# A hand-ordered two-attention decoder block: the last two groups of the first attention packed closer, batch 0's second maxima set behind them, batch 1's middle stage set earlier

## What is computed

```python
x = x + attn(layernorm(x))        # 16 heads of 8, scores = q.k + q.pe_k[clip(j-i)], softmax,
                                  # ctx = attn.v + attn.pe_v[clip(j-i)], then W_out and bias
y = layernorm(x)
# new memory = ctx_1024 shifted against y: a convolution (rate 4) over the old memory, then y itself
x = x + cross(ctx_1024, y)
src = layernorm(x)
# the block: q, k, v by W_q, W_kc W_k, W_vc W_v, rotary embedding, softmax(q.k), W_o, rmsnorm,
# a shared swiglu and 8 experts in 2 groups (the best group, its top 2), rmsnorm
x = x + ffn(src)
```

## Time and profile before

| what | value |
|---|---|
| median of 3 runs | 417.42 us (417.29 to 420.8) |
| profiled execution | 415.42 us, span 413.6 us, 1.8 us around it |
| PE busy | 356.1 us (86% of the span) |
| DVE busy | 297.4 us (72%) |
| ACT busy | 232.8 us (56%) |
| POOL busy | 162.4 us (39%) |
| mean granted clock of PE | 0.92 of full speed |

### The profile page before, as it was taken

One profiled execution on the slowest core, in us unless ns is written; L12 is line 12 of the kernel. 1 busy time (PEld: TensorE's weight loads), 2 busy tenths in 40 slices (PEclk: granted clock), 3 DMA queues, 4 the chain that ended last, 5 costly groups with the idle time before them and its releaser, 6 DMA issues.

```text
span 413.6 us, 12788 instructions
## 1 busy us (share of the span) xinstructions
PE 356.1 (86%) x5267; PEld 188.8 (46%) x5267; DVE 297.4 (72%) x538; ACT 232.8 (56%) x489; POOL 162.4 (39%) x342
## 2 busy tenths in 40 slices
PE   7667789898999999897889898769989898899993
PEld 4233356675676677654555332311333333453441
DVE  5998747777678788788799789566787661436465
ACT  2724656767666757565744567455867695422200
POOL 7264555456477576554470111200001161143423
PEclk9995559999999999999999699965999899999997
DMA  7400000000000001000000000500000000000000
GB/s 235 133 22 4 4 4 5 6 4 6 23 7 4 6 6 30 4 4 2 3 5 2 4 24 2 164 3 1 2 2 1 2 3 2 0 1 0 2 25 26
DMA packets 11991, 8.08 MB, mean 20 GB/s; under 512 B 4446, under 2 KB 11022, under 8 KB 11806
## 3 DMA queue, kind: packets, MB, share of 16 engines
q1 hardware_dynamic: 11934, 7.27, 6.1%
HBM read 5.94 MB, written 0.52 MB: 16 GB/s over the span
## 4 chain that ended last, share of the span: by engine, by line
PE 57%; DVE 22%; issue 7%; ACT 6%; POOL 3%; SPq 2%; DMA 2%; ACTq 0%; POOLq 0%; DVEq 0%
PE ps L1213 8%; PE ps L1308 7%; PE ps L1127 5%; PE ps L1158 5%; PE ps L1176 5%; DVE m_qk L850 4%; PE ps L1139 4%; PE ps L1185 4%; PE ps L1200 3%; PE ps L1097 3%; PE ps L1003 3%; ACT arena L683 3%; DVE m_qk L847 2%; PE ps L1294 2%; SPq L383 2%
## 5 line engine op out<-in xcount | busy, mean ns | idle before, releaser
L847 DVE TENSOR_REDUCE m_qk<-ps 128x2 f32<-128x1024 f32 x64 | 76.8, 1220 | 19.5 <-PE ps L1097 19.3
L850 DVE TENSOR_REDUCE m_qk<-ps 128x2 f32<-128x1024 f32 x64 | 76.9, 1219 | 15.9 <-PE ps L1185 15.5
L683 ACT ACTIVATE arena<-ps 128x512 f32<-128x512 f32 x128 | 69.4, 594 | 23.5 <-PE ps L1139 22.8
L698 ACT ACTIVATE arena<-ps 128x512 f32<-128x512 f32 x128 | 67.2, 590 | 21.2 <-PE ps L1200 20.9
L598 POOL TENSOR_TENSOR arena<-arena,eb 128x256 f32<-128x256 f32 x64 | 47.0, 734 | 62.4 <-ACT eb L671 31.6
L671 ACT ACTIVATE eb<-ps 128x512 f32<-128x512 f32 (+1 forms) x64 | 31.3, 542 | 30.3 <-PE ps L1127 30.3
L441 POOL TENSOR_SCALAR var<-mv 128x1 f32<-128x1 f32 (+1 forms) x14 | 2.7, 193 | 106.3 <-ACT eb L740 69.8
L1213 PE MATMUL ps<-arena,v_sb 128*20 128x256 f32 x512 | 41.2, 415 | 2.4 <-DVE arena L855 2.4
L1158 PE MATMUL ps<-arena,v_sb 128*20 128x128 f32 x1024 | 40.3, 284 | 0.0
L599 POOL TENSOR_TENSOR arena<-arena,eb 128x192 f32<-128x192 f32 x64 | 38.6, 603 | 0.0
L1200 PE MATMUL ps<-q_op,k_op 50*128 50x512 bf16 x128 | 31.9, 414 | 4.8 <-ACT arena L698 4.0
(11 more groups left out here) (217 smaller groups left out, 523.8 us busy)
## 6 DMA issues: line engine op xcount, KB each, us to landing
rel_v<-in_relv_ext SPq DMA_DIRECT2D x1, 1024.0 KB, 8.9
eb<-in_w SPq DMA_DIRECT2D x2, 512.0 KB, 5.3
x_sb<-in_x SPq DMA_DIRECT2D x2, 256.0 KB, 3.2
q_op<-farT SPq DMA_DIRECT2D x32, 3.0 KB
q_op<-farT SPq DMA_DIRECT2D x32, 1.5 KB
out<-x_sb SPq DMA_DIRECT2D x8, 64.0 KB, 1.5
rows<-in_rows SPq DMA_DIRECT2D x1, 448.0 KB, 6.7
sel<-in_sel SPq DMA_DIRECT2D x1, 384.0 KB, 4.2
```

Source lines behind the costliest of these rows:

```text
L683: act.activation(p_ring[:, k % SLOTS_P, e, :], ps[:, bank, :], ACT.Exp).then_inc(sm["bank_free"], 1)
L698: act.activation(p_ring[:, v % RING, e, :], ps[:, bank, :], ACT.Exp).then_inc(sm["bank_free"], 1)
L847: dve.tensor_reduce(m_qk[:, u, n:H:PAIRS], ps[:, banks, :], AX_X, ALU.max).then_inc(sm["pair_free"], 1)
L850: dve.tensor_reduce(m_qk[:, IT * b + n, 2 * p:2 * p + 2], ps[:, banks, :], AX_X, ALU.max).then_inc(sm["pair_free"], 1)
```

## The change

Only numbers of the plan change; every step is still there once, with the same instructions.

- Group 7: `bias` at 8, 9.5, 11, 12.5 (before 8, 11, 14, 17), `scores` one each step from 15 to 22 (before 15 to 25), `pv` from 21.6 to 25 (24 to 28), `crel` from 25.6 (29), and its `turn`, `fin`, `norm`, `back` some 5.5 steps sooner. Group 6: `crel` from 30.3 in steps of 0.7 (before 31 in steps of 1). Group 5: `fin`, `norm`, `back` ten steps sooner (97 and not 107).
- Batch 0: the four `again` six steps later (from 104.8 and not 98.5), `max2` from 108.5 (before 102.6), `sc2` from 118.5 (116).
- Batch 1: the middle stage from 116 (122), `max2` from 140.5 (139), `sc2` from 150.5 (147.5).
- `FRONT_AT` (output projection and gates of batch 0) 154.5 (152) and `LAST` 186.5 (183.5), three steps later with the end of `sc2`.

```diff
+BIAS_LAST = (8, 9.5, 11, 12.5)
+SCORES_LAST = (15, 16, 17, 18, 19, 20, 21, 22)
+CREL_EARLY = (30.3, 31, 31.7, 32.4)
...
-PV_LAST = (24, 24, 25, 25, 26, 26, 28, 28)
-MID_AT = (78, 122)
-MAX2_AT = (102.6, 139)
-SC2_AT = (116, 147.5)
+PV_LAST = (21.6, 21.6, 22.2, 22.2, 23, 23, 25, 25)
+CREL_LAST = (25.6, 26.2, 26.8, 27.4)
+MID_AT = (78, 116)
+MAX2_AT = (108.5, 140.5)
+SC2_AT = (118.5, 150.5)
 PV2_LAST = (1, 1.5, 2, 2.5, 3, 3.5, 4, 4.5)
-FRONT_AT = 152
-LAST = 183.5
+FRONT_AT = 154.5
+LAST = 186.5
...
+        bias_at, scores_at, pv_at = (BIAS_AT, SCORES_AT, PV_AT) if u < NT - 1 else (BIAS_LAST, SCORES_LAST, PV_LAST)
+        crel_at = CREL_AT if u < NT - 2 else (CREL_EARLY, CREL_LAST)[u - NT + 2]
+        plan += [(t + bias_at[q], 2, "bias", u, q) for q in range(4)]
+        plan += [(t + scores_at[p], 2, "scores", u, p) for p in range(PAIRS)]
         plan += [(t + pv_at[k], 6, "pv", u, k) for k in range(8)]
-        plan += [(t + CREL_AT[q] - early, 7, "crel", u, q) for q in range(4)]
-        plan += [(t + 35 - early, 0, "ctx", u, 0)]
+        plan += [(t + crel_at[q], 7, "crel", u, q) for q in range(4)]
+        plan += [(t + crel_at[3] + (1 if u < NT - 2 else 0.5), 0, "ctx", u, 0)]
         if u == NT - 1:
-            plan += [(t + 33.6, 1.5, "turn", u, 0), (t + 34.2, 5, "fin", u, 0), (t + 35.5, 1.5, "norm", u, 0), (t + 37, 4, "back", u, 0)]
+            plan += [(t + 28.2, 1.5, "turn", u, 0), (t + 28.8, 5, "fin", u, 0), (t + 29.8, 1.5, "norm", u, 0), (t + 31.2, 4, "back", u, 0)]
         else:
             plan += [(t + 36, 1.5, "turn", u, 0)]
-            t += 37 if u % IT >= IT - 2 else 47
+            t += 37 if u % IT >= IT - 2 or u == NT - 3 else 47
...
-    plan += [(t + d, 4, "again", 0, 2 * k) for k, d in zip((0, 2, 1, 3), (20.5, 21.6, 22.7, 23.8))]
+    plan += [(t + d, 4, "again", 0, 2 * k) for k, d in zip((0, 2, 1, 3), (26.8, 27.8, 28.8, 29.8))]
```

More of the change, by code:

```diff
@@ L122, in relative_plan @@
         plan += [(t + 4, 4, "rel_rows", u, 0), (t + 7, 4, "far_rows", u, 0), (t + 12, 4, "qk_rows", u, 0)]
-        plan += [(t + BIAS_AT[q], 2, "bias", u, q) for q in range(4)]
-        plan += [(t + SCORES_AT[p], 2, "scores", u, p) for p in range(PAIRS)]
-        pv_at, early = (PV_AT, 0) if u < NT - 1 else (PV_LAST, 2)
+        bias_at, scores_at, pv_at = (BIAS_AT, SCORES_AT, PV_AT) if u < NT - 1 else (BIAS_LAST, SCORES_LAST, PV_LAST)
+        crel_at = CREL_AT if u < NT - 2 else (CREL_EARLY, CREL_LAST)[u - NT + 2]
+        plan += [(t + bias_at[q], 2, "bias", u, q) for q in range(4)]
+        plan += [(t + scores_at[p], 2, "scores", u, p) for p in range(PAIRS)]
         plan += [(t + pv_at[k], 6, "pv", u, k) for k in range(8)]
-        plan += [(t + CREL_AT[q] - early, 7, "crel", u, q) for q in range(4)]
-        plan += [(t + 35 - early, 0, "ctx", u, 0)]
+        plan += [(t + crel_at[q], 7, "crel", u, q) for q in range(4)]
+        plan += [(t + crel_at[3] + (1 if u < NT - 2 else 0.5), 0, "ctx", u, 0)]
         if u == NT - 1:
-            plan += [(t + 33.6, 1.5, "turn", u, 0), (t + 34.2, 5, "fin", u, 0), (t + 35.5, 1.5, "norm", u, 0), (t + 37, 4, "back", u, 0)]
+            plan += [(t + 28.2, 1.5, "turn", u, 0), (t + 28.8, 5, "fin", u, 0), (t + 29.8, 1.5, "norm", u, 0), (t + 31.2, 4, "back", u, 0)]
         else:
             plan += [(t + 36, 1.5, "turn", u, 0)]
-            t += 37 if u % IT >= IT - 2 else 47
+            t += 37 if u % IT >= IT - 2 or u == NT - 3 else 47
             plan += [(t, 5, "fin", u, 0), (t + 2, 1.5, "norm", u, 0), (t + 4, 4, "back", u, 0)]
```

## The result

The changed kernel took 430.44 us in the median (424.64 to 434.23, 4 runs) beside 417.36 us of the kernel before; the ratio is 1.0256, with a 95% interval of 1.0194 to 1.0319. The ratios leave out runs of the slower state (over 1.5% above the kernel's fastest), so they are not those of the medians. So the change makes the kernel 2 to 2.6% slower, by the ratios 9 to 11 us. Forecast were +4.7 us and a range of 413 to 428.5 us: the sign was right, the size half of what came. The ratio of 1.0256 on 417.4 us gives 428.1 us, just inside the range; the median of 430.4 us lies above it, that of the second timing (425.5 us) inside.

The account below looks back on a forecast made before the run. PE, busy 86% of the span, was taken as the nearer bound, with DVE at 72%. The terms -5 + 10.7 - 1 gave +4.7 us, so 422 us, with an 8-in-10 range of 413 to 428.5 us.

Parts of the forecast that it names:

- Part 1: Close of the first attention: 9 us more PE work before the first max2, which comes 11 us later, at about 213.
- three waits that I named: PE waits at the first attention's close: some 2 us at back 4, 0.7 at back 5, 1.3 at pv 7.0.
- Part 2: First max2 to first sc2: maxima alone, DVE the bound; first sc2 at about 231.5, 8.4 us later than before.
- Part 3: From first sc2 to batch 1's last turn, with 9.5 us of DVE waits: turn ends about 277, 5 us sooner.
- the hole is filled: Rival: batch 0's maxima fill the waits of batch 1's projections; -6.8 us, 410.6 us in all; chance 18%.
- Part 4: After batch 1's last turn: PE has 10.7 us more left to do, less 1 us of losses.
- Part 1's waits: Up to the first max2: new PE waits of 4 to 4.5 us replace the 3.4 us lost in 191 to 202.
- the term for the clock: After batch 1's last turn: losses from waits and half clock fall 3.5 us at most or grow 2; taken as 1 less.
- the clock stays low: Rival: PE at half clock from 224 until the turns are over; 427 to 430 us; chance 15%.
- the clock rule: Ties clock drops to idle gaps between matmul bursts; the maxima piece would keep full clock, first pv2 steps some 2 us sooner.
- the row: Profile of before at 230 to 232: clock fell to half with no idle gap over 0.55 us; drop expected among the maxima.

Follow-up runs that it names:

- second timing: The changed kernel, unaltered, timed and profiled once more with more runs: 425.5 us, ratio 1.0209 to the kernel before.
- C alone: Only the close-up of groups 5 to 7 kept from the change, all else as in the kernel before: ratio 1.0067.
- e1: The changed kernel with batch 0's turns, maxima and sc2 and batch 1's middle stage put back, keeping only the close-up of groups 5 to 7: 421.36 us, ratio 1.0067.
- e2: Close-up of groups 5 to 7 plus batch 1's earlier middle stage; batch 0's turns, maxima and sc2 as in the kernel before: 418.23 us, ratio 1.0016.
- D alone: The kernel before with only batch 0's turns, maxima and sc2, and what follows them, set later: 421.22 us, ratio 1.0111.
- e3: The changed kernel with batch 1's middle stage back at 122: 424.78 us, ratio 1.0168 to the kernel before.
- e4: The changed kernel with norm 4 ahead of the second split on DVE and ctx 6 ahead of the first turn on ACT: 427.49 us, ratio 1.0161.
- e5: The changed kernel with PE making the products of batch 0's first 16 second maxima twice: 429.31 us, ratio 1.0282 to the kernel before.
- e7: The changed kernel with 16 useless matmuls ahead of batch 1's first turn: 427.72 us, ratio 1.0255 to the kernel before.
- e6: e2 with fin, norm and back of group 5 ten steps later, as before the change: 418.38 us, ratio 0.9990 to the kernel before.
- e10: The changed kernel with e4's two edits and useless matmuls ahead of all of batch 1's turns: 422.64 us, ratio 1.0136 to the kernel before.
- e11: e6 with useless matmuls ahead of batch 1's turns, 6 then 4 each: 417.96 us, ratio 1.0008 to the kernel before.
- e12: The kernel before with only batch 0's turns, maxima and sc2, and what follows them, set later; repeated with more runs: 421.22 us, ratio 1.0111.

## Why the prediction was half right

**Part 1, the close.** The three waits that I named came: 2.00, 0.73 and 1.33 us stand where 2, 0.7 and 1.3 were forecast, and C alone with the turns in their place suffers from the same chain (3.62 us in e1, 3.63 in e2). But they were not all of the waits, see below. The first `max2` came 12.8 us later than before in the second profile (218.37, less the 3.47 us by which that profile was late at `xT`), forecast 11, and 14.6 later in the first. I had written that PE gains nothing by this part; e1 shows that it costs 0.7%.

**Part 2, maxima alone.** Held in kind: 18.55 us from the first maximum to the first `sc2`, forecast 18.5 (19.46 in the first profile); DVE busy 87%, where I had said over 90%, PE 80% busy where I had said under 65%, since it worked at half clock and took longer over the same. D alone costs 1.1%. The clock fell inside the piece, as forecast, but it was back at full speed when `pv2` started (0.63 us for its first row in both profiles, 1.06 at half clock), where I had it low.

**Part 3, to the last turn.** Forecast 5 us sooner than before; it was 3.0 sooner in the second profile (282.55 - 3.47) and not at all in the first (284.55 - 2.44 = 282.1). The stage itself held: from the first `sc2` to the end of the last turn 45.6 and 45.9 us, forecast 45.5. It began too late for the forecast, and `y` of batch 1 came 4.2 and 1.5 us sooner than before (counted from `xT`), not 5.5. DVE idles 8.5 of 34.2 us from the first `pv2` to there, 2.0 of 11.5 from `sc2` to `pv2`: 10.5 us where I took 9.5. The maxima did fill DVE, as the rival "the hole is filled" wanted, but what they fill is the list that PE then waits for, 4.53 us ahead of the first turn.

**Part 4, what is left.** From the last turn to the last `pv2` 76.85 us in the second profile, 9.3 more than before; forecast 9.7. In the first, with the clock at 0.89 and not 0.96, 81.1 us, 13.5 more.

**The step that failed** is the size of two terms. The first is Part 1's waits, "Together 4 to 4.5 us in place of the 3.4 us lost in 191 to 202". From `xT` to the first `max2`, before and in the second profile:

```profile
177.04:202.09 25.05, 21.12 (x416) 12.74 (x413) 19.53 (x32) 16.68 (x34) 10.41 (x16) 1.00 0.01 3
```

```profile
180.51:218.37 37.86, 30.17 (x685) 19.84 (x682) 20.90 (x38) 23.79 (x47) 20.42 (x32) 1.00 0.02 3
```

PE's own work grew by 9.05 us, forecast 9. Its idle time went from 3.9 to 7.7 us. The 3.4 us that I took off held 1.4 us of waits at batch 0's turns (0.44, 0.76 and 0.17), and those did not go: 0.33, 0.53 and 0.84 us are there now, with 0.65 and 0.21 at `scores`. In the second profile this term is nearly the whole miss of the sum: the stretch grew by 6.3 us where 4.7 was forecast, 1.8 of it too much in Part 1 and all other parts within 0.5 us.

The second is the term for the clock: "The losses can fall by 3.5 us at most ..., or grow by 2 us ... I take 1 us less". It held in the second profile and not in the first, where Part 1 also lost 2.0 us of work to half clock and Part 4 came out 3.8 us too long. Over the runs, the estimate above has +5.2 us at equal clock and 3.5 us more that go with the clock, where I had subtracted 1. I had read the clock's drops as places in the list, two of them in the changed stretch, which move along with their steps. In the runs its level goes with PE's idle time: every kernel here in which PE idled 26.7 us and more in the stretch ran at a median clock of 0.883 to 0.898 (the changed one, e3, e4, e5, e7); those with under 25 us at 0.907 to 0.913 (the kernel before, e1, e2, e6, e10, e11); D alone, 25.3 us, at 0.901. That the waits lower it is not shown by this. All kernels of the first group hold C and D, the idle time is from one profile each, and the mean clock is over the whole span, whose first 177 us already differ from run to run (0.90 before, 0.89 and 0.87 in the two profiles of the changed kernel). The rival "the clock stays low", 427 to 430 us, has the median of the changed kernel's runs beside it (425.5 and 430.4), though the place that I named, the piece of the maxima, is probably not where it is lost: e5 kept PE busier there and gained nothing. Where the clock's share is lost is not settled; e7 kept it up at the turns in one profile and gained nothing in the median.

*On the clock rule cited in the prediction (the Trainium skill, "TensorE: Matmul & The Clock Gate", section "Why this matters for your kernels"): the piece of the maxima had 0.71 and 0.77 of the clock in two profiles with no single wait over 1.42 us in the first and 1.11 in the second, so there the row was the better guide. Behind the wait of 4.53 us the clock fell in both, as the rule says. In the first it fell once more at 285, behind waits of 1.54 and 0.86 us.*

## What to carry to other kernels

Work of two engines that runs side by side at full load (here 19.6 and 19.5 of 21.1 us) is the last thing to pull apart: closing up one attention and putting the maxima behind it made PE wait 6.6 us more, and the middle stage moved under them gave none of it back (29.7 us beside 28.6). Before filling a hole with an idle engine's work, ask whether that engine's next result is what ends the hole. And where the clock's level moves by hundredths from run to run, it helps to compare a change at equal clock too, and by the idle time of PE, which two profiles of one kernel gave as 29.7 and 29.8 us while their lengths differed by 7 us.

## What the runs showed that I had not expected

- The time of one and the same kernel follows the mean granted clock by 2.5 to 2.75 us for each hundredth; over 49 runs on three chips the kernel before went from 414.2 to 426.8 us. The differences begin before anything differs: 177.04, 179.48, 180.51 and 182.04 us to the same `xT` with the same order.
- Waits of 2.00, 0.64 and 0.21 us were followed by half clock in one profile (200 to 207), and waits of 2.01, 0.65 and 0.21 us by full clock in the other.
- Where a `tensor_tensor` of DVE and one of POOL, both of 128x512, met in batch 1's second projection, the one that began second took longer. In the changed kernel POOL began 0.14 us ahead: it took 1.16 us and DVE 1.57, where DVE takes 0.69 for the same operation on the first projection. In `e12` (and alike in e2 and e3) DVE began 0.04 us ahead: it kept its 0.69 us, and POOL took 1.67. From the changed kernel:

```profile
261.56 0.69 DVE L937 TENSOR_TENSOR part<-part,rest 128x512 f32<-128x512 f32 x1
...
265.11 1.57 DVE L937 TENSOR_TENSOR part<-part,rest 128x512 f32<-128x512 f32 x1
```

```profile
264.97 1.16 POOL L345 TENSOR_TENSOR part<-rest,part 128x512 bf16<-128x512 f32 x1
```

From `e12`:

```profile
266.39 0.69 DVE L932 TENSOR_TENSOR part<-part,rest 128x512 f32<-128x512 f32 x1
```

```profile
266.43 1.67 POOL L340 TENSOR_TENSOR part<-rest,part 128x512 bf16<-128x512 f32 x1
```
